# Scaling the queries on VectorE instead of ScalarE, with GpSimd's and ScalarE's lists reordered around it

## What is computed

```
xa = layernorm(x)
q = rms_norm(xa @ q_w.T + q_b) * norm_q_w            # 16 heads of 32
k = rms_norm(ctx @ k_img_w.T + k_img_b) * norm_k_img_w
v = ctx @ v_img_w.T + v_img_b
x = x + tanh(g_xattn) * (softmax(q k^T / sqrt(32)) v @ o_w.T + o_b)
h = layernorm(x)
y = square(relu(h @ up_w)) @ down_w + (h @ expert_weight) * (sum of the 2 largest of h @ gate_w)
x = x + tanh(g_ffn) * (layernorm(y) * ln_gamma + ln_beta)
```

## Time and profile before

| what | value |
|---|---|
| median of 3 runs | 1372.42 us (1371.9 to 1376.5) |
| the profiled execution's own time | 1372.42 us |
| its span (first to last instruction) | 1370.6 us |
| mean granted clock of TensorE | 0.996 |
| TensorE busy | 1334.5 us, 97% |
| VectorE / ScalarE / GpSimd busy | 65% / 45% / 38% |

### The profile page before, as it was taken

How to read it: one execution, slowest core, us unless ns; L and a number is a source line. 1 busy time by engine, 2 the same in 40 slices (tenths; PEclk the granted TensorE clock), 3 DMA queues, 4 the chain that set the end, 5 groups by cost and what they waited for, 6 DMA issues and landing times.

```text
span 1370.6 us, 27962 instructions
## 1 busy us (share of the span) xinstructions
PE 1334.5 (97%) x9264; PEld 1139.9 (83%) x9264; DVE 893.7 (65%) x1739; ACT 614.1 (45%) x1891; POOL 524.2 (38%) x671
## 2 busy tenths in 40 slices
PE   6899999999999999999999999999999999999996
PEld 5688888888888888898888888888888888888884
DVE  5555555555555655887776785775775776776764
ACT  4777777777777777532312212322213113223210
POOL 3566666666665776433131131140140140240211
PEclk9999999999999999999999999999999999999998
DMA  6133333333333311448549449458368468367541
GB/s 232 55 99 109 107 107 107 107 107 111 120 113 96 104 63 41 160 140 204 180 147 253 144 154 252 130 154 254 125 164 250 138 168 249 116 177 222 174 144 36
DMA packets 215091, 199.15 MB, mean 145 GB/s; under 512 B 126321, under 2 KB 126449, under 8 KB 215025
## 3 DMA queue, kind: packets, MB, share of 16 engines
q1 hardware_dynamic: 182768, 139.57, 34.9%
q10 hardware_dynamic: 32256, 58.73, 12.8%
HBM read 156.32 MB, written 41.94 MB: 145 GB/s over the span
## 4 chain that ended last, share of the span: by engine, by line
PE 81%; issue 8%; DVE 5%; POOL 1%; ACT 1%; ACTq 0%; DVEq 0%; POOLq 0%
PE bank L75 16%; PE bank L77 16%; PE bank L76 16%; PE wide L76 7%; PE wide L77 7%; PE wide L75 7%; PE bank L340 4%; PE bank L302 3%; PE wide L318 2%; PE wide L352 2%; ACT prob L641 1%; DVE c L1298 1%; POOL yrstd L1790 1%; PE wide L1491 1%; PE wide L1488 1%
## 5 line engine op out<-in xcount | busy, mean ns | idle before, releaser
L1565 ACT ACTIVATE hT_hi<-c 128x512 fp32r<-128x512 f32 x128 | 79.9, 631 | 402.9 <-PE wide L77 210.1
L641 ACT ACTIVATE prob<-wide,nmx 128x128 f32<-128x128 f32 x512 | 182.3, 403 | 103.4 <-DVE nmx L466 100.1
L1797 POOL TENSOR_TENSOR pair<-pair,beta 128x512 f32<-128x512 f32 x28 | 37.5, 1339 | 451.3 <-DMA pair<-x_scratch 451.3
L76 PE MATMUL wide<-wo_lo,hT_hi 128*128 128x512 f32 x512 | 203.3, 397 | 0.0
L77 PE MATMUL wide<-wo_hi,hT_lo 128*128 128x512 f32 x512 | 201.9, 394 | 0.0
L75 PE MATMUL wide<-wo_hi,hT_hi 128*128 128x512 f32 x512 | 201.5, 394 | 0.0
L801 POOL TENSOR_TENSOR prob<-prob,rr 128x512 f32<-128x512 f32 x128 | 138.3, 1081 | 94.9 <-DVE rr L474 92.0
L1643 DVE TENSOR_TENSOR hT_lo<-c,hT_hi 128x512 fp32r<-128x512 f32 x128 | 99.2, 795 | 75.6 <-ACT hT_hi L1565 74.8
L641 ACT ACTIVATION_READ_ACCUMULATOR prob<-wide,nmx 128x1 f32 x512 | 124.0, 242 | 0.0
L77 PEld LDWEIGHTS wide<-wo_hi,hT_lo 128*128 128x128 f32 x512 | 96.1, 188 | 22.7
L75 PEld LDWEIGHTS wide<-wo_hi,hT_hi 128*128 128x128 f32 x512 | 96.2, 188 | 21.5
(11 more groups left out here) (226 smaller groups left out, 3548.7 us busy)
## 6 DMA issues: line engine op xcount, KB each, us to landing
wo_hi<-ring_scratch ACTq DMA_DIRECT2D x110, 256.0 KB, 3.7
wo_lo<-ring_scratch ACTq DMA_DIRECT2D x110, 256.0 KB, 4.5
wo_hi<-ring_scratch SPq DMA_DIRECT2D x46, 256.0 KB, 2.7
wo_lo<-ring_scratch SPq DMA_DIRECT2D x46, 256.0 KB, 2.9
fx<-x_scratch SPq DMA_DIRECT2D x36, 256.0 KB
xin<-in_x SPq DMA_DIRECT2D x32, 256.0 KB, 2.6
cin<-in_ctxT SPq DMA_DIRECT2D x32, 256.0 KB, 2.8
xres<-in_x SPq DMA_DIRECT2D x32, 256.0 KB, 4.0
```

The costliest lines, as they stand in the source:

```text
L76: eng.matmul(dst, ah, bl, start=False, stop=False)
L641: i = act.activation(prob[par][:, g, h * P:(h + 1) * P], cols(bank[g], h), ACT.Exp, bias=nmx[:, n:n + 1], scale=1.0, accum_out=rs[:, n:n + 1])
L1565: return act.activation(dst, src, ACT.Copy)
```

## The change

- `scale_q` leaves ScalarE. VectorE makes `qf` with a `tensor_scalar` between `inverse(s, 3)` (in slot -1: after `normalise`) and `residual_sum(o)`; TensorE waits for VectorE's semaphore instead.
- On ScalarE `hi_ctx(n + 1)` moves to where `scale_q` was, ahead of `take_probs(a, 3)` and `take_kT`.
- On GpSimd `inv_rms_q(n)` moves behind `divide(s, 3)`, and in slot -1 behind the first `weight_lo`.
- In `drain` VectorE does `sums_all` and `squares` ahead of the low parts of the up weights, and the third of these (128x1024) goes to GpSimd's end of the drain.

```diff
@@ TensorE, slot
-                        at_least(pe, ac_qf, n + 1)
+                        at_least(pe, dv_qf, n + 1)
@@ VectorE, slot
                     if has(n + 1) and not has(a):
                         normalise(n + 1, par)
+                    if has(n):
+                        at_least(dve, po_rq, n + 1)
+                        dve.tensor_scalar(qf[:, :], qb[:, :], rq[:, 0:1], None, ALU.mult).then_inc(dv_qf, 1)
                     if has(o):
                         residual_sum(o, par, BO)
@@ VectorE, drain
                     split_values(s)
+                    ff.sums_all(dve, 0, 0)
+                    ff.squares(dve, 0, 0)
                     ff.up_lo(dve, 1, 0)
                     ff.up_lo(dve, 1, 1)
-                    ff.sums_all(dve, 0, 0)
-                    ff.up_lo(dve, 1, 2)
-                    ff.squares(dve, 0, 0)
                     residual_sum(s, s % 2, BO_S)
@@ ScalarE, slot -1 and slot
-                def scale_q(n):
-                    at_least(act, po_rq, n + 1)
-                    act.activation(qf[:, :], qb[:, :], ACT.Copy, scale=rq[:, 0:1]).then_inc(ac_qf, 1)
-                        scale_q(0)
                         weight_hi(2, 1)
                         take_qT(0)
@@
-                    scale_q(n)
+                    if has(n + 1):
+                        hi_ctx(n + 1, par)
                     if has(a):
                         take_probs(a, 3)
                     take_kT(n)
-                    if has(n + 1):
-                        hi_ctx(n + 1, par)
@@ GpSimd, slot -1
                         inv_std(1)
+                        weight_lo(2, 0)
                         inv_rms_q(0)
-                        weight_lo(2, 0)
                         weight_lo(2, 1)
@@ GpSimd, slot
+                    divide(s, par, 3)
                     inv_rms_q(n)
-                    divide(s, par, 3)
                     if has(a):
                         residual(a, 1 - par)
@@ GpSimd, drain
                     residual(s, s % 2)
+                    ff.up_lo(pool, 1, 2)
```

More of the change, by code:

```diff
@@ L131, in flamingo_layer @@
                 sem("pe_" + n) for n in ("K", "Q", "Tx", "TP", "PV", "Tk", "Tq", "S", "O"))
[L132 to L135, removed]
+            dv_kb, dv_qb, dv_kf, dv_qf, dv_xT, dv_aT, dv_vb, dv_mx, dv_rr, dv_bs, dv_st, dv_xn, dv_p = (
+                sem("dv_" + n) for n in ("kb", "qb", "kf", "qf", "xT", "aT", "vb", "mx", "rr", "bs", "st", "xn", "p"))
+            ac_sk, ac_sq, ac_xT, ac_pT, ac_aT, ac_kT, ac_qT, ac_c, ac_e = (
+                sem("ac_" + n) for n in ("sk", "sq", "xT", "pT", "aT", "kT", "qT", "c", "e"))
             po_mk, po_rk, po_mq, po_rq, po_c, po_r, po_var, po_rs, po_p = (
```

## The result

The changed kernel takes 1414.74 us (median of 4 runs, 1414.61 to 1415.16), the kernel before 1373.09 in the runs beside it: ratio 1.030, 95% interval 1.0281 to 1.0319. Forecast were 1409.0 us with a range of 1390 to 1420, and slower with 0.93. The profiled execution took 1416.72 us with a span of 1414.9, 2 us above the median.

What follows compares the result with a forecast made beforehand. TensorE's list was taken to bound the steady slots, so the change could only delay it. Steady slots 29.1, start and slot 30 6.0, drain 1.5: 36.6 us on 1372.4, giving 1409.0 us, range 1390 to 1420.

Steps and rivals of the forecast that it cites:

- TensorE bound, only lateness counts, `xn`'s turn the tight place: Steady slots: TensorE's list sets 16.55 us; the change can only be late, tightest at `xn`'s turn, with 0.93 us spare.
- The port conflict between `qf` and `xres`: Steady slots: `qf` starts 0.06 us after GpSimd's `xres`, waits for it on the shared port, and delays `residual_sum`.
- ends 0.28 after `xres`: Steady slots: the blocked `qf` ends 0.28 us after `xres`, making TensorE's turn of `xn` reciprocal end + 4.29.
- Written-out slots, 0.97 each: Slots 2, 17 to 23 and 25 to 29: `xn`'s turn 0.97 us later in each, 12.6 us in all.
- Loop slots, 1.26 and 1.10: Seven odd loop slots 1.26 us longer each (8.8), seven even ones 1.10 each (7.7).
- Start and slot 30, 6.0: Slots -1, 0 and 30: late turns of `qf` (2.5, 2.2, 0.2) and low clock (1.1) cost 6.0 us, bounds 2.6 and 7.5.
- The lower bound, 2.6: Start and slot 30: the least cost; without the blocking, slots -1 and 0 would lose 1.6 and 1.0.
- the low clock: Slot -1: after 4.1 us of TensorE idling, some 3 us of mostly matmuls run at half speed, costing 1.1 (0 to 1.5).
- The drain, 1.5: Drain: GpSimd's 128x1024 difference meets VectorE's both-in-SBUF sums, making low parts late for TensorE; 1.5 us (0 to 2.6).
- VectorE wins: Port: VectorE wins or nothing blocks; slots lose 0.01 written-out, 0.29 odd, 0.13 even; 1378 us in all; chance 0.08.
- Twice blocked: Slots: `qf` is blocked by `xres` and then by `lo_ctx`, 1.25 us more in 27 slots, 1443; chance 0.05.
- the rival on the other side: Slot 1: shorter lists end TensorE's waits and low clock; with the port conflict absent, 1368 us; chance 0.02.

Runs made afterwards that it cites:

- Number 5: The changed kernel with all its reordering, but `qf` stays on ScalarE behind `take_kT`, in slot -1 too: 1383.56 us.
- (2): The changed kernel with GpSimd's `inv_std(s+3)` moved between `rq` and `residual`, so `qf` has another neighbour: 1395.77 us.
- number 3: The changed kernel with GpSimd's `residual` split into two instructions of 256 columns: 1398.5 us.
- number 9: The changed kernel with a one-column `tensor_scalar` on GpSimd between `rq` and `residual`: 1385.84 us.
- number 6: The kernel before with only the three drain edits of the change: 1381.51 us, against 1375.01 for the kernel before on the same chip.
- number 10: The changed kernel with `residual_sum` ahead of `qf`, the old drain, and slot -1's power ahead of both `weight_lo`: 1379.4 us.
- number 11: The changed kernel with a one-column `tensor_scalar` ahead of GpSimd's `residual`, slot -1's power first and the old drain: 1382.93 us, ratio 1.0073 to the kernel before.
- 7: The changed kernel with `residual_sum` ahead of `qf` and the drain of the kernel before: 1382.01 us.

## Why the prediction was right, point by point

- **TensorE bound, only lateness counts, `xn`'s turn the tight place**: shown. Number 5 has all of the reordering with `qf` on ScalarE, and slots of 16.55.
- **The port conflict between `qf` and `xres`**: shown three ways: by removing the neighbour (2), by halving it (3), and by changing who starts first (9). The step "ends 0.28 after `xres`" came out at 0.29, and 0.28 for the two-operand sum in the drain. A block of the whole instruction, as the Trainium skill words it (SBUF — State Buffer, section Who interferes with whom), would be about 0.2 us longer than these rows show (0.49 alone against 0.28 from the release). That one fully waits and the earlier one wins agrees with all of these runs. By the recorded starts has an exception, `xn`, which lost although 0.08 us ahead, so the trace's order of two near starts doesn't tell the winner.
- **Written-out slots, 0.97 each**: 0.98 measured (17.53 - 16.55), 13 of them; slot 24 free, as forecast.
- **Loop slots, 1.26 and 1.10**: mis-sized. Measured 1.50 and 1.27, and 1.72 in slot 3; the 14 together 19.5 us instead of 16.5. Two things were left out. TensorE goes on 0.24 us after `residual_sum` in the loop (14.03 after 13.79 in slot 4), 0.10 in the written-out slots, while I took 0.06 for all. And in the odd slots the reciprocal that starts the chain came 0.10 later than before, 0.28 later in slot 3. The trace puts this on ScalarE: in slot 5 VectorE's first maximum starts at the same moment (1.41 us after the scores, 1.40 before), but the first exponential starts at 2.30 instead of 2.19, and what follows is late by as much. With `qf` on ScalarE (5) it is 2.20. Why ScalarE starts later, no run tested.
- **Start and slot 30, 6.0**: 6.2 for the start, from the scores of slot 2 (61.87 before, 68.09 after), and 0.3 in slot 30 from a turn of `qf` at 13.08 instead of 12.76. The turn of slot -1 came at 26.65 (26.6 forecast), with 4.06 us of idle TensorE, and in slot 0 the wait is 2.53. The lower bound, 2.6, was summed too low: in slot 0 the turn of an unblocked `qf` comes 1.2 later by the prediction's own terms (40.0 + 0.57, against 39.38), not 1.0, and 1.2 in number 9. The clock fell where it was expected, and again in slot 0, which was not. Windows of the changed kernel, slots -1, 0 and 1:

```profile
22.00:26.60 4.60, 0.59 (x3) 0.15 (x1) 2.00 (x2) 1.83 (x5) 3.24 (x4) 1.00 0.55 191
...
28.00:31.00 3.00, 3.00 (x8) 2.14 (x7) 2.08 (x4) 1.49 (x3) 1.43 (x2) 0.50 0.00 0
...
45.00:51.00 6.00, 5.17 (x41) 4.19 (x42) 3.94 (x8) 3.16 (x6) 0.79 (x2) 0.50 0.26 89
...
62.00:65.00 3.00, 3.00 (x39) 2.54 (x32) 2.81 (x4) 1.09 (x3) 2.92 (x4) 0.50 0.03 5
```

  TensorE did 0.59 us of work in 4.60, and then 3.00 of matmuls at 0.50, the level of 1.2 GHz. Counted from the turn of `kf`, the first scores come after 8.56 us in the kernel before, 8.15 in number 6 with the same start, and 11.98 in the changed kernel. 2.6 of these 3.4 lie ahead of the turn of `qf`. Behind it the kernel before and number 10, both at the full clock, take 4.61 and 4.60 to the scores, the changed kernel 5.41: so 0.8 is the low clock, forecast as 1.1. Slot 0 then is 2.5 longer and slot 1 0.25. The clock is the part that varies between runs. In number 11, with number 10's order and a turn at 24.98, it was at 0.50 from 26 to 29 all the same; in numbers 3 and 9 the stretch from the turn of `qf` to the scores takes 6.5 and 6.6.
- **The drain, 1.5**: mis-sized, 2.5 measured in two kernels (6 and the changed one). The mechanism was the one told. After it comes another 0.9 us to the logits' turn in the changed kernel's profile, and about 2 us more are spread over the feed-forward part, in which nothing was changed; the timed runs are 2 us below the profiled one. From the last block's scores to the end the profiles of the four kernels with the old drain (before, 7, 10, 11) take 829.0 to 830.6 us, those of the nine with the new one 831.6 to 835.4. Less the drain's own 2.5 the latter are 829.1 to 832.9, so some runs pay up to 3.8 us more behind it and some nothing; why, stays open.
- **The rivals**: "VectorE wins" is what number 9 made happen, and slot 17 then is 16.55, as worked out; its loop slots cost 0.50 (odd) and 0.26 (even), 0.72 in slot 3 and 0.39 in slot 4, not 0.29 and 0.13, mostly for the reasons above. "Twice blocked" fell with number 3 and with the changed kernel's own rows: `lo_ctx` takes 1.45 instead of 1.28, behind `qf`. The low clock in slot 1 stayed (last row above), so the rival on the other side gained nothing. Its size was about right: in numbers 3 and 9 the clock stayed at 1.00 behind the waits of slot 1, which lasted 19.56 us instead of 21.15. Number 11, with number 9's lists in the slots, had the low clock there and 22.10 us, so the lists don't decide it.

## What to carry to other kernels

Before an elementwise operation is moved to a less busy engine, ask which instruction of the engine that shares its port starts with it, and what stands behind it in the new list: here 0.5 us of work became 1.5, and the price was paid by the instruction behind it, which frees a PSUM bank. Where two such instructions are released by the same event, their order can be chosen, by swapping lists or by a small operation in between that holds the other back far enough (0.21 us did, 0.03 did not). And where the steady part is as long as one engine's list, as here, rebalancing the others had nothing to win and something to lose.

## What the runs showed of the hardware that was not expected

- The winner is decided on a fine scale: `qf` 0.03 us behind `xres` loses 1.0 us, 0.14 ahead it loses nothing and costs GpSimd 0.21 (1.49 instead of 1.28). `xn` in the earlier trace rows lost while recorded 0.08 ahead.
- From the end of `residual_sum` to the turn TensorE takes 0.24 us in the hardware loop and 0.10 in the written-out slots, where the same wait ends last in both. That the loop's wait, against a counter instead of a constant, is the reason was not tested by itself.
